# Testing for firing neurons on the halved inputs, without the two voltage scans

## The reference, cut to what matters

```python
def lif(x):                      # x: batch, time, channel; TAU = 2, VTH = 1
    def step(v, xt):
        v = v + (xt - v) / TAU
        s = spike(v - VTH)       # 1 where v >= 1
        return (v * (1.0 - s), s)
    _, sT = lax.scan(step, zeros, xT)
...
x = x + lif(time_mix(layer_norm(x, ln1_s, ln1_b), ...))
x = x + lif(channel_mix(layer_norm(x, ln2_s, ln2_b), ...))
```

## Time and profile before

| what | value |
|---|---|
| median of 3 runs | 690.81 us (690.18 to 691.85) |
| the profiled execution's own time | 692.57 us |
| its span, first to last instruction | 690.4 us |
| mean granted TensorE clock | 0.973 |
| busy share: PE, DVE, ACT, POOL | 86%, 86%, 78%, 65% |
| instructions: PE, DVE, ACT, POOL | 2241, 1596, 849, 576 |
| DMA, mean over the span | 25 GB/s |

### The profile page before, as it was taken

How to read it: one execution, slowest core, us unless ns; L and a number is a source line. 1 busy time by engine, 2 the same in 40 slices (tenths; PEclk the granted TensorE clock), 3 DMA queues, 4 the chain that set the end, 5 groups by cost and what they waited for, 6 DMA issues and landing times. The chain is left out here.

```text
span 690.4 us, 10811 instructions
## 1 busy us (share of the span) xinstructions
PE 594.9 (86%) x2241; PEld 368.2 (53%) x2241; DVE 591.0 (86%) x1596; ACT 536.2 (78%) x849; POOL 445.8 (65%) x576
## 2 busy tenths in 40 slices
PE   1247479999999989999899989999999999989883
PEld 0023136565656647565566646575656565656662
DVE  2875969999999979999899979999999999975631
ACT  4845367988979887979689887979797988858672
POOL 4332454697778666877678766868778684745352
PEclk9998679999999999999999999999999999999997
DMA  6110010001010100101010100001010101000000
GB/s 217 61 31 2 0 31 16 17 17 31 17 31 17 32 2 16 30 16 31 16 30 16 30 16 23 9 15 31 16 31 1 32 2 31 16 1 16 1 16 15
DMA packets 26553, 16.93 MB, mean 25 GB/s; under 512 B 1152, under 2 KB 25728, under 8 KB 26240
## 3 DMA queue, kind: packets, MB, share of 16 engines
q1 hardware_dynamic: 26496, 16.34, 7.8%
HBM read 12.14 MB, written 4.19 MB: 24 GB/s over the span
## 5 line engine op out<-in xcount | busy, mean ns | idle before, releaser
L782 ACT ACTIVATE hid<-p_f,scale 128x512 f32<-128x512 f32 x128 | 88.0, 687 | 70.1 <-PE p_f L1739 69.7
L1739 PE MATMUL p_f<-a_lo,w_hi 128*128 128x512 f32 x320 | 132.9, 415 | 2.9 <-DVE a_lo L295 1.7
L1739 PE MATMUL p_f<-a_hi,w_hi 128*128 128x512 f32 x320 | 125.8, 393 | 0.0
L1739 PE MATMUL p_f<-b_lo,w_hi 128*128 128x512 f32 x256 | 112.0, 438 | 4.0 <-DVE b_lo L295 3.0
L1739 PE MATMUL p_f<-b_hi,w_hi 128*128 128x512 f32 x256 | 100.5, 393 | 0.0
L776 ACT ACTIVATE a_hi<-hid 128x512 fp32r<-128x512 f32 x128 | 79.1, 628 | 12.0 <-DVE hid L1269 10.3
L429 POOL TENSOR_TENSOR rstd<-var,minus_half 128x4 f32<-128x4 f32 x64 | 84.3, 1318 | 2.5
L445 POOL TENSOR_TENSOR nd<-factors,pq 128x512 f32<-128x512 f32 x32 | 39.2, 1226 | 56.5 <-DVE pq L1129 56.4
L295 DVE TENSOR_TENSOR a_lo<-hid,a_hi 128x512 fp32r<-128x512 f32 x96 | 64.0, 691 | 11.2 <-ACT a_hi L776 11.0
L1739 PEld LDWEIGHTS p_f<-a_lo,w_hi 128*128 128x128 f32 x320 | 60.2, 188 | 22.6 <-issue 7.5
L1724 PE MATMUL p_m<-kk,mix 128*128 128x512 f32 x128 | 66.3, 625 | 3.8 <-issue 3.8
(11 more groups left out here) (141 smaller groups left out, 1501.3 us busy)
## 6 DMA issues: line engine op xcount, KB each, us to landing
xa<-in_x SPq DMA_DIRECT2D x16, 256.0 KB, 2.8
xb<-in_x SPq DMA_DIRECT2D x16, 256.0 KB, 3.1
out<-y_out SPq DMA_DIRECT2D x16, 256.0 KB, 3.0
kk<-in_ffn SPq DMA_DIRECT2D x1, 1024.0 KB, 6.3
hid<-in_ffn SPq DMA_DIRECT2D x1, 1024.0 KB, 8.8
mix<-in_mix SPq DMA_DIRECT2D x1, 512.0 KB, 6.5
gate<-in_ffn SPq DMA_DIRECT2D x1, 512.0 KB, 4.0
mix<-in_mix SPq DMA_DIRECT2D x1, 320.0 KB, 3.8
```

The lines of the kernel that those rows point to most:

```text
L782: act.activation(hid[:, m], p_f[m % 2][:, :], ACT.Gelu, scale=scale[:, 1 + layer, m:m + 1]).then_inc(s_gelu[layer], 1)
L1739: last = pe.matmul(out_, w[:, b], x[:, k], start=(k == 0 and t == 0), stop=(k == n - 1 and t == len(terms) - 1))
```

## The change

`voltage` is gone for both layers, with the tiles `volt` and the semaphores `s_volt`. `fire(k)` reads the halved inputs themselves and compares them with 0.5: layer 0 in PSUM (`p_k`), layer 1 in SBUF (`h_in[1]`). If no halved input reaches a half, no voltage can reach one, so nothing fires; if one does, the flag is set and POOL's step loop decides as before. Whoever waited for `s_volt[0]` (ACT's copy and PE's two products into `p_k`) now waits for `s_fired[0]`. The order of all other calls stays; in `turn` and `last_turn` the call `voltage(0)` stood between `fire(1)` and `fired_flag(1)`.

```diff
             def neuron_input_1(g):
                 act.wait_ge(s_wo, g.n + 1)
-                act.wait_ge(s_volt[0], g.n + 1)
+                act.wait_ge(s_fired[0], g.n + 1)
...
-            def voltage(k, g):
+            def fire(k, g):
 
                 if k == 0:
                     dve.wait_ge(s_wo, g.n + 1)
                 else:
                     dve.wait_ge(s_h_in[k], g.n + 1)
-                for b in range(NB):
-                    fed = h_in[k][:, b] if k else p_k[:, b * T:(b + 1) * T]
-                    last = dve.tensor_tensor_scan(volt[k][:, b], half_row[:, :], fed, 0.0, ALU.mult, ALU.add)
-                last.then_inc(s_volt[k], 1)
-
-            def fire(k, g):
-
-                dve.wait_ge(s_volt[k], g.n + 1)
                 wait(dve, s_spk_tok[k], g.n)
                 wait(dve, s_spikes[k], g.n)
-                dve.tensor_scalar(spikes[k][:, :, :], volt[k][:, :, :], 1.0, None, ALU.is_ge, ALU.add,
+                fed = flat(h_in[k][:, :, :]) if k else p_k[:, :]
+                dve.tensor_scalar(flat(spikes[k][:, :, :]), fed, 0.5, None, ALU.is_ge, ALU.add,
                                   accum_out=fired[k][:, :]).then_inc(s_fired[k], 1)
...
                 if on[3]:
-                    voltage(1, g[3])
                     fire(1, g[3])
-                if on[2]:
-                    voltage(0, g[2])
-                if on[3]:
                     fired_flag(1, g[3])
                 if on[2]:
                     fire(0, g[2])
...
                 def k_product(g):
 
                     after(pe, s_h_in[0], g.n - 1)
-                    after(pe, s_volt[0], g.n - 1)
+                    after(pe, s_fired[0], g.n - 1)
```

More of the change, by code:

```diff
@@ L138, in build @@
         h_in = [sb(f"h_in{k}", [P, NB, T]) for k in range(2)]
-        volt = [sb(f"volt{k}", [P, NB, T]) for k in range(2)]
         spikes = [sb(f"spikes{k}", [P, NB, T], BF16) for k in range(2)]
@@ L247, in build @@
         s_h_in = [sem(f"s_h_in{k}") for k in range(2)]
-        s_volt = [sem(f"s_volt{k}") for k in range(2)]
         s_fired = [sem(f"s_fired{k}") for k in range(2)]
```

## The result

| what | before | after |
|---|---|---|
| median of the runs | 691.33 us (4 runs) | 679.38 us (4 runs, 677.72 to 680.32) |
| the profiled execution's own time, its span | 692.57, 690.4 us | 677.72, 675.9 us |
| mean granted TensorE clock | 0.973 | 0.962 |

What follows compares the result with a forecast made beforehand. Each turn was taken as bound by DVE from `add_1` to `low(1, 3)`, then PE to the transposes, plus DVE's instruction-fetch stalls. Gains of 9.8 + 1.1 + 1.5 = 12.4 us from 690.81 gave 678.4 us, range 676 to 689.

Steps and rivals of the forecast that it cites:

- The loop's stall: DVE's loop, shortened to fit three instruction blocks, no longer stops at the backward branch: 9.8 us gained, bounds 0 and 10.5.
- Rival 1: DVE's loop: the stops at the backward branch stay, only 1.1 + 1.5 us remain, 688.2 us; chance 0.12.
- The scans' work: DVE: removing 64 scans, 43.0 us, gains 0 in steady turns, since DVE then waits for PE.
- rival 2: DVE is the bound and its 43 us count, at most 35 us over 16 turns: 656 us; chance 0.03.
- one ring: Steady turn of 36.87 us: DVE from `add_1` to `low(1, 3)`, then PE from `hidden(1)` to the transposes; scans in neither.
- POOL beside the scans: POOL's `norm_5`, ahead of `neurons(1)`, gets shorter without scans, so `spikes_turned(1)` waits less: 1.5 us, bounds 0 and 1.5.
- The filling turns: First turns: PE's four waits for `fire`, 4.8 us, shrink; 1.1 us gained, bounds 0 and 4.8.
- The comparison from PSUM, and ACT's copy: Layer 0's comparison takes 0.7 us, hidden; ACT's copy comes 0.3 us late, taken up by its wait ahead of `gelu(1, 3)`: 0.
- Rival 3: ACT's late copy delays `high(2, 1)`, then DVE's `low(2, 1)` and `add_1` in 14 turns: up to 700.8 us; chance 0.05.

Runs made afterwards that it cites:

- the padded kernel of before: The unchanged kernel, all scans kept, with 60 idle instructions at the head of DVE's list: 681.41 us, ratio 0.9857.

## Why the prediction was right, point by point

**The loop's stall** (9.8 us). Right in place, cause and size: the three steps with a branch gave 9.3, and the padded kernel of before, which removes the stall alone, gained 10.0. The 0.5 between 9.8 and 9.3 is the step that served as the measure: the prediction took 36.41 us, the step that leaves the loop, and that one still takes 36.38; the steps with a branch take 36.56 to 36.57. By the section "Instruction fetch mechanics" of the Trainium skill's page "Runtime: NRT & Kernel Launch", a taken branch to something outside of what the engine holds waits for a fetch; the traces agree, 2.4 to 3.6 us each time. The page's blocks of 256 instructions are not what these runs show: the packets come one at a time, 8 KB each, where blocks of 128 have their edges. The place of the stall alone would fit either size, and the sum of 9.8 didn't need the choice.

**Rival 1** (the stall stays, 688.2) fell in the changed kernel. Brought back by 24 idle instructions it gives 683.7: its size isn't fixed, and the prediction's 3.5 us belonged to the old place of the branch.

**The scans' work, term 0, and rival 2** (DVE is the bound). Of 43 us of DVE work gone, 37 came back as waiting ahead of `fired_flag`. With all scans or with layer 1's alone, turns 4 to 17 take the same time (479.3 and 479.2 us), so layer 0's 20.2 us cost nothing in their old place. The prediction's reason was half of the picture: it named one ring, with DVE from `add_1` to `low(1, 3)` as its long half. With 1.05 us taken out of that half the turn stayed as long, where some 668 us should have come out; with PE's list shortened it stayed as long too. The reading that fits is two loops of nearly the same length. The term was right because the scans lie in neither. The 35 us of rival 2 were out of reach. The Trainium skill's page "Perfetto Trace Analysis" (section "Identifying the Most-Contended Engine") would start at the busiest engine; DVE was as busy as any, and taking 43 us off it gave some 2 us beside the stall, so the runs don't bear the rule out for this work.

**POOL beside the scans** (1.5 us). Right, in size and for the most part in mechanism: 1.8 between turns 4 and 17 with layer 1's scans alone, 1.2 of it in turns in which the transposes come late behind POOL, 0.44 in one in which they don't. `norm_5` fell from 859 to 681 ns per instruction (3.60 to about 2.75 per group), as forecast. It is layer 1's scans, whose input comes from SBUF, that do this; `shift_1` shows that layer 0's, with theirs from PSUM, don't.

**The filling turns** (1.1 us). Its size stays open. The waits themselves went as forecast: PE waits for `fire` 1.3 us in all where it waited 4.8. What that was worth can't be read. The two profiled executions differ by 4.2 us by turn 4, but traces of the changed kernel's code start there anywhere between 111.04 and 114.09, and the kernels with all scans at 114.59, 116.27 and 117.01. The medians can't settle it either: 691.33 to 679.38 is 11.95, the stall and POOL take 9.8 + 1.5 to 10.0 + 1.8, and the 0.2 to 0.7 that is left is less than the interval of 1.7. So that the sum of 12.4 comes within 0.5 of the measured 11.95 is in part luck: its smallest terms are under what these runs resolve.

**The comparison from PSUM, and ACT's copy** (0 each). The comparison takes 692 ns. ACT's copy comes 1.14 us after PE's sum (402.10 to 403.24) where it came 0.78 after it, so 0.36 late for 0.3 forecast, and moving it back changed the time by 0.3 us, less than the scatter.

**Rival 3** (slower through the late copy, 700.8) didn't happen, but its mechanism and its place are shown: with the copy 1.08 us later (2.22 against 1.14 behind the sum) the kernel takes 699.2. Its price was set too low. By the prediction 0.3 of the 1.08 would be free and the rest cost 0.8 us a turn; measured are 1.7.

## What to carry to other kernels

An engine that stands on "issue" at the first instruction of a hardware loop, with packets of instructions near it, may be waiting for its own code, as it was here: count its instructions from branch to branch and where they lie in the blocks, and try padding ahead of the loop before touching the work. Busy shares of 86% on two engines say that neither is surely the bound; the start of the consumer against the end of each producer says more, and even that named only one of the loops here; shortening each side in turn showed the other. When an intermediate that another engine waited for is cut out, look at what that engine waits for now: here layer 0's scans cost nothing in one place and 20 us in the next.

## What the runs showed that I had not expected

- The stall at the backward branch had two sizes: 3.4 to 3.6 us with the branch 5 instructions past the edge, 2.4 to 2.7 with 7 and with 25. Why isn't shown.
- 60 idle instructions at the head of the list made a kernel 10.0 us faster, and nothing in the trace shows a price for them.
- Of two kinds of scan on DVE, the one with its input from SBUF lengthens POOL's elementwise work beside it (`norm_5` from 681 to 846 ns on average, `shift_1` from 1.04 to 1.40 us), the one with its input from PSUM leaves `shift_1` at 1.04.
- The granted clock in the filling turns differs from one execution to the next (0.56, 0.50 and 0.82 in the same ten microseconds), and with it the start of turn 4 of the same code, by 3 us, more than most of the terms one argues about.
- A DVE instruction of 0.68 us took 1.60 (from 1.54 to 1.61) in each of twelve turns in which a like one on POOL had begun 0.22 to 0.30 us ahead of it.
